# Local attention of a two-layer block: masks added in the pass that takes the maxima, key rotation sum on GpSimd, output product one unit later

## The reference

```python
h = shift_token(x)                       # half of the features from the token before
q, k, v = split(h @ wqkv)                # 8 heads of 64
q = l2norm(q) * qs;  k = l2norm(k) * ksc
q, k = rotary_xpos(q, k)                 # q * cos * scale + rotate_half(q) * sin * scale
# blocks of 128 queries look at 256 keys: their own block and the one before
sim = einsum('bhwid,bhwjd->bhwij', q * 8, k)
mask = (i < j) | (i > j + 128) | (j == -1)
attn = softmax(where(mask, -max, sim))
x = x + (attn @ v) @ wo
```

## Time and profile before

| | |
|---|---|
| median of 3 runs | 3439.26 us |
| the profiled execution's own time | 3436.8 us |
| its span | 3435.1 us |
| PE busy | 3159.2 us, 92% |
| DVE busy | 1936.2 us, 56% |
| ACT busy | 1575.8 us, 46% |
| POOL busy | 724.3 us, 21% |
| mean granted TensorE clock | 0.958 |

### The profile page before, as it was taken

The page is one execution under the profiler, slowest core; times in us unless marked ns, Lnnn a source line. Parts: engine busy times, 40 slices in busy tenths (PEclk is TensorE's granted clock), DMA queues, the critical chain, the costliest instruction groups (busy, mean ns, idle before and its releaser), DMA issues. The chain is left out here.

```text
span 3435.1 us, 46202 instructions
## 1 busy us (share of the span) xinstructions
PE 3159.2 (92%) x15128; PEld 1817.9 (53%) x15129; DVE 1936.2 (56%) x4725; ACT 1575.8 (46%) x3537; POOL 724.3 (21%) x861
## 2 busy tenths in 40 slices
PE   8899998977999969999987999997998999997998
PEld 4455555544666623333324666664555666665555
DVE  6999994541111126666645878773223777775322
ACT  5666652211222226666654666662222656564221
POOL 0000003560000045555532322220001111110111
PEclk9999998998999969999998999998999999998999
DMA  4000004012111111111002000000001000000000
GB/s 145 1 1 1 1 0 167 28 58 92 45 45 44 43 41 28 28 32 30 22 15 65 10 9 10 10 5 27 0 0 34 9 10 8 10 6 4 13 13 25
DMA packets 81274, 97.37 MB, mean 28 GB/s; under 512 B 14611, under 2 KB 68263, under 8 KB 80811
## 3 DMA queue, kind: packets, MB, share of 16 engines
q1 hardware_dynamic: 74106, 76.65, 6.9%
q0 software_dynamic: 6960, 18.10, 1.7%
HBM read 60.35 MB, written 24.13 MB: 25 GB/s over the span
## 5 line engine op out<-in xcount | busy, mean ns | idle before, releaser
L2302 PE MATMUL ps_loc_psa<-sb_stk_w,sb_loc_hT 128*128 128x512 f32 x768 | 350.1, 606 | 5.3 <-DMA sb_stk_wo<-in_loc_wo 3.6
L1706 DVE CUSTOM_DVE_ANT_0 sb_win_masked<-ps_win_pss,sb_win_around 128x384 f32<-128x384 f32 (+1 forms) x512 | 256.3, 538 | 175.0 <-PE ps_win_pss L1801 174.8
L2589 PE MATMUL ps_mlp_ps<-sb_mlp_hT,sb_stk_w 128*128 128x512 f32 (+1 forms) x768 | 322.5, 613 | 22.2 <-DVE sb_mlp_hid L2542 22.2
L2099 ACT ACTIVATE sb_loc_pr<-ps_loc_psw,sb_loc_nb,sb_loc_sc 128x256 f32<-128x256 f32 x512 | 281.0, 569 | 114.4 <-DVE sb_loc_nb L2227 114.4
L1801 PE MATMUL ps_win_pss<-sb_win_kT,sb_win_q 32*128 32x384 f32 (+1 forms) x1024 | 235.2, 531 | 38.1 <-DVE sb_win_qtok L1706 35.7
L1612 ACT ACTIVATE sb_win_pT<-ps_win_pst 128x512 f32<-128x512 f32 x368 | 199.8, 595 | 124.4 <-PE ps_win_pst L1812 122.3
L2542 DVE SCALAR_TENSOR_TENSOR sb_mlp_hid<-ps_mlp_ps,sb_stk_col,sb_mlp_gl 128x512 f32<-128x512 f32 x96 | 71.7, 749 | 303.3 <-ACT sb_mlp_gl L2511 303.3
L2511 ACT ACTIVATE sb_mlp_gl<-ps_mlp_ps,sb_stk_col 128x512 f32<-128x512 f32 x96 | 65.9, 687 | 381.7 <-PE ps_mlp_ps L2589 381.5
L2302 PEld LDWEIGHTS ps_loc_psa<-sb_stk_w,sb_loc_hT 128*128 128x128 f32 x768 | 142.1, 192 | 181.6 <-issue 177.7
L2589 PEld LDWEIGHTS ps_mlp_ps<-sb_mlp_hT,sb_stk_w 128*128 128x128 f32 (+1 forms) x768 | 130.3, 184 | 201.4 <-issue 201.4
L709 PE MATMUL ps_rec_psp<-sb_rec_hT,sb_rec_w 128*128 128x512 f32 x512 | 235.4, 604 | 0.8 <-DVE sb_keep_modf L466 0.8
(11 more groups left out here) (313 smaller groups left out, 6468.1 us busy)
## 6 DMA issues: line engine op xcount, KB each, us to landing
sb_exp_rows<-sorted_tokens SPq DMA_DIRECT2D x72, 128.0 KB, 2.0
expert_results<-sb_exp_res SPq DMA_DIRECT2D x72, 128.0 KB, 1.7
sb_moe_w_in<-in_L_ffn_w_in_eDF SPq DMA_DIRECT2D x8, 512.0 KB, 11.3
sb_moe_w_sw<-in_L_ffn_w_swiglu_eDF SPq DMA_DIRECT2D x8, 512.0 KB, 11.4
sb_exp_w_out<-in_L_ffn_w_out_eFD SPq DMA_DIRECT2D x8, 512.0 KB, 7.1
sb_win_sums<-sb_win_raw SPq DMA_DIRECT2D x128, 32.0 KB, 2.0
sb_stk_angles<-in_angles SPq DMA_DIRECT2D x32, 128.0 KB, 3.8
out_y<-sb_stk_y SPq DMA_DIRECT2D x8, 512.0 KB, 2.9
```

Source lines behind the costliest of these rows:

```text
L1706: nc.vector.tensor_tensor_reduce(masked[:, pair % 2, j, 0:keys], pss[:, (n + j) % PLAIN, 0:keys], around[:, first:first + keys], 1.0, -3e3 ...
L2099: e = nc.scalar.activation(pr[:, hf, h], psw[:, hf, h // 2, h % 2 * 256:h % 2 * 256 + 256], ACT.Exp, scale=sc8[:, b, hh:hh + 1], bias=nb[: ...
L2302: t = nc.tensor.matmul(psa[:, c], hT[:, b, k, 1 - k:P + 1 - k], w[:, k, c * 512:(c + 1) * 512], start=(k == 0), stop=(k == KD - 1))
L2589: i = nc.tensor.matmul(ps[at:at + M, q % 2, i2], w1[:, k, i2 * HID + f * P:i2 * HID + f * P + M], hT[:, b, k], start=(k == 0), stop=(k == ...
```

## The change

Four things are edited, all within `local_attention` and its tiles.

1. `masks` is removed from TensorE, and with it the bf16 identity. The mask is an f32 tile now. `maxima` is one `tensor_tensor_reduce` for each of the four heads of a half: it adds the mask to the scores in PSUM, writes the sum into `pr` in SBUF, and takes the maximum. The exponentials read `pr` and write it in place.
2. The sum of the keys' two rotated parts goes from VectorE (end of `rotate_keys`) to GpSimd (`add_keys`, behind `add_queries`). `rotate_keys(i)` waits for the sum of the tile before.
3. TensorE's `output(i)` moves from behind `turn_keys(i + 1)` to the next tile, between `project(i + 2)` and `turn(i + 1)`.
4. VectorE's `add_output(i)` moves behind `rotate_keys(i + 2)` of the next tile.

```diff
@@ gpsimd
+                def add_keys(i):
+                    j, b, _ = at(i)
+                    pool.wait_ge(s_krot, F + i + 1)
+                    kr = t1[:, b, INNER:]
+                    nc.gpsimd.tensor_tensor(kr, kr, t2[:, INNER:], ALU.add).then_inc(s_krope, 1)
...
                 for i in range(TILES):
                     if i + 1 < TILES:
                         add_queries(i + 1)
+                        add_keys(i + 1)
                     spread_sums(i)
@@ scalar, exps
-                        e = nc.scalar.activation(pr[:, hf, h], psw[:, hf, h // 2, h % 2 * 256:h % 2 * 256 + 256], ACT.Exp,
+                        e = nc.scalar.activation(pr[:, hf, h], pr[:, hf, h], ACT.Exp,
@@ vector, rotate_keys
                     dve.wait_ge(s_k, F + i + 1)
+                    if F + i:
+                        dve.wait_ge(s_krope, F + i)
...
                     i2.then_inc(s_krot, 1)
-                    dve.wait_ge(s_krot, F + i + 1)
-                    kr = t1[:, b, INNER:]
-                    nc.vector.tensor_tensor(kr, kr, t2[:, INNER:], ALU.add).then_inc(s_krope, 1)
@@ vector, maxima
+                    form = 0 if j == 0 else 2 - (j + 1) % 2
                     dve.wait_ge(s_s, n + 1)
-                    nc.vector.tensor_reduce(top[:, hf], psw[:, hf].rearrange("p a (h n) -> p (a h) n", h=2), AX_X,
-                                            ALU.max).then_inc(s_top, 1)
+                    if F + i:
+                        dve.wait_ge(s_tp, n - 1)
+                    else:
+                        dve.wait_ge(s_masks, 16)
+                    for h in range(4):
+                        t = nc.vector.tensor_tensor_reduce(pr[:, hf, h], psw[:, hf, h // 2, h % 2 * 256:h % 2 * 256 + 256],
+                                                           mask[:, form], 1.0, -3e38, ALU.add, ALU.max, top[:, hf, h:h + 1])
+                    t.then_inc(s_top, 1)
@@ vector, loop
                         rotate_keys(i + 1)
+                    if i:
+                        add_output(i - 1)
                     invert_sums(i)
...
                         copy_keys(i + 1)
-                    add_output(i)
...
+                add_output(TILES - 1)
@@ tensor, scores (masks is gone)
                     pe.wait_ge(s_kT, F + i + 1)
+                    if i:
+                        pe.wait_ge(s_riT, F + i)
...
-                                                     kT[r:r + LHD, b, hh // 2].rearrange("p s n -> p (s n)"), start=False,
+                                                     kT[r:r + LHD, b, hh // 2].rearrange("p s n -> p (s n)"), start=(h == 0),
@@ tensor, loop
                         project(i + 1, 2, s_v)
+                    if i:
+                        output(i - 1)
                     turn(i, 0)
...
                         turn_queries(i + 1)
-                        masks(i + 1)
                         turn_keys(i + 1)
-                    output(i)
                     if i + 2 < TILES:
                         turn_input(i + 2)
+                output(TILES - 1)
```

More of the change, by code:

```diff
@@ L1896, in local_attention @@
     ident, x, y, xs_b = keep["ident"], keep["x"], S["y"], S["xs_b"]
-    w, wo, scl, angles, mask, identb = (S[n] for n in ("w", "wo", "scl", "angles", "mask", "identb"))
+    w, wo, scl, angles, mask = (S[n] for n in ("w", "wo", "scl", "angles", "mask"))
     L, sem = layer, S["loc"]
@@ L2017, in _ @@
                 if L == 0:
-                    for dst, name in ((mask, "loc_mask"), (identb, "ident")):
-                        pool.dma_start(dst[:], a[name]).then_inc(s_masks, 16)
+                    pool.dma_start(mask[:], a["loc_mask"]).then_inc(s_masks, 16)
                 nc.gpsimd.memset(v[:, :, 1], 0.0).then_inc(s_pad, 1)
@@ L2030, in _ @@
                 add_queries(0)
+                add_keys(0)
                 tables(1)
@@ L2320, in turn_keys @@
                     t.then_inc(s_kTp, 1)
[L2322 to L2331, removed]
                 def scores(i):
@@ L2394, in _ @@
                 turn_keys(0)
-                if L == 0:
-                    pe.wait_ge(s_masks, 32)
-                masks(0)
                 for i in range(TILES):
@@ L2623, in local_stack @@
             "angles": m.sb("angles", [P, RING, 2, 2, LHD]),
-            "mask": m.sb("mask", [P, 3, 2 * P], BF16),
-            "identb": m.sb("identb", [P, P], BF16),
+            "mask": m.sb("mask", [P, 3, 2 * P]),
             "w": m.sb("w", [P, KD, 3 * INNER]),
```

## The result

The changed kernel takes 3490.72 us (median of 4 runs, 3488.43 to 3496.14), against 3439.57 us for the kernel before on the same chip (4 runs, 3437.61 to 3440.13). The ratio is 1.0152, 95% interval 1.0134 to 1.0170: slower by 51 us, 10 us more than was forecast, and within the range. The profiled execution took 3496.1 us, its span 3494.4 us.

The account below looks back on a forecast made before the run. TensorE's stream was taken as the bound before, the values-to-keys chain after. Thirty steps of +0.78 us (23.4), less 2.2 at the ends, gave 21.2 a layer, 42.4 for two: 3481 us, range 3462 to 3506.

Parts of the forecast that it names:

- The chain from the values' end to usable keys: Behind the values, scaling output and keys, turning and copying keys take 2.97 us; no next scores can start sooner.
- The two idle times: TensorE waits per tile: about 1.0 us ahead of the keys' turn, 0.6 to 0.7 ahead of the scores.
- The step, 16.25, and 16.39 with the additions: Scores to scores in a local-attention tile: 16.25 us against 15.61, 0.64 longer, or 0.78 longer with small terms.
- spreading: GpSimd's spreading of the sums, late behind the output's addition and reciprocal on VectorE, adds 0.06 us a step.
- restart: Scores that start after a wait run slightly longer: 0.08 us a step, bound 0 to 0.2.
- Maxima, exponentials, keys' sum: hidden: First part of a tile: four reductions, exponentials from SBUF and the keys' sum on GpSimd add 0 to the step.
- The ends of a layer, -2.2: Per layer: first scores earlier (-0.86), first step (-0.6), last step's difference (+0.3), last tile (-1); together -2.2 us.
- the first step, -0.6: The first step of a layer has no output in it: 15.0 us for 15.61, so -0.6.
- The last tile, -1: Output falls into TensorE's wait for the last tile's exponentials, and the clock may hold: -1 us, between 0 and -2.5.
- The clock falls at each tile: Rival: two close waits with only turns between cost the full clock, 1.5 us or more a step, 3575; chance 0.08.
- Rival 1, TensorE stays the bound: The saving of 1.04 us a step is kept, step 14.57, total 3372, if the chain is below 2.33; chance 0.08.
- What bounds the kernel now: Local attentions: TensorE, busy for all but 0.4 of 400 us, sets the 15.61 us step; better overlap wins nothing there.

Follow-up runs that it names:

- `masks_only`: Kernel before with only the masks moved to VectorE (in the maxima, no mask products, exponentials from SBUF); ratio 1.0015.
- `out_moved_only`: Kernel before with only the output product and its addition moved to the next tile, masks still on TensorE; ratio 1.0106.
- `out_back`: Changed kernel with the output product and its addition back in their old places; ratio 1.0085.
- `after_again`: Changed kernel, unedited, run once more on another chip; ratio 1.0159 to the kernel before.
- `filler`: Changed kernel with two unused f32 products, about 0.86 us, on TensorE in the wait ahead of the keys' turn; ratio 1.0119 to the kernel before.
- `after_keys_first`: Changed kernel with VectorE scaling the keys ahead of the output; ratio 1.0079 to the kernel before.
- `before_chain_short`: Kernel before, masks still on TensorE, with keys scaled ahead of the output, input turned ahead of the keys, layer 0's normalising late; ratio 0.9960.
- `keys_back`: Changed kernel with only the keys' sum back on VectorE; ratio 1.0146 to the kernel before.
- `after_keys_first_modulate_late`: Changed kernel with keys scaled ahead of the output and, in layer 0, ScalarE's normalising at the end of the tile; ratio 1.0028 to the kernel before.

## Why the prediction was right, point by point

- *The chain from the values' end to usable keys, 2.97 us, becomes the bound.* Right. It is 3.01. `masks_only` and `out_moved_only` show that its two parts are two waits. The keys' turn comes 1.53 us behind the values' end with or without masks, so their removal gains nothing. The scores come at 3.0 to 3.1 once the output no longer stands between, and its move costs the step. The two idle times were forecast as about 1.0 and 0.6 to 0.7 us; they are 0.88 and 0.61.
- *The step, 16.25, and 16.39 with the additions.* It is 16.31. The additions *spreading*, 0.06, and *restart*, 0.08, do not show: the sums' turns follow those of the exponentials after 1.91 as before, and the scores last 1.93. In their place the scores start 0.10 behind the copy, not 0.05. So +0.70 a step, not +0.78.
- *Maxima, exponentials, keys' sum: hidden.* Right for the change: pitch of the reductions 0.35, the exponentials end 1.26 us early. *Keys' sum* is hidden only since the output is ahead of the turns; in `out_back` it costs 0.36.
- *The ends of a layer, -2.2.* Mis-sized. The first scores do come earlier, by 0.77 (0.83 us behind the start of the keys' copy, it was 1.60). But *the first step, -0.6*, is +1.84 in layer 1 and +1.42 in layer 0: its scores run at 1.2 GHz, which costs 1.70 by the rows. The earlier trace rows had been read as scores that could simply start earlier; that the masks ran at the slow clock ahead of them was not seen. That the missing output itself saves what was said is shown by `out_moved_only`, where the masks stand ahead of the scores and the first step is 14.7, 1.66 us under its other steps. *The last tile, -1*: -0.90 in layer 1 from the last scores to the MLP's first transposes, 0.0 in layer 0, where the last scores ran at the slow clock (3.61 for 1.93).
- *The clock falls at each tile* was a rival that excluded the forecast. In truth it is a term of the sum: it falls in 4 steps of 31 a layer in the profiled execution, 6.6 us, and in one and two in `after_again`. This term was left out, because the case was treated as all or nothing. The prediction named a clock below 1.00 in the stretch as a sign of being wrong, and it is 0.99: for this part it was. Whether transposes alone would let the clock fall, as the rival has it, no run separates: `filler` put products where TensorE had been idle.
- *The sum.* Profiled: from the first scores to the last +29.3 and +29.7 us, with the ends +28.5 and +28.0 a layer, 56.5 together; 2.8 of the 59.3 us by which the profiled executions differ lie outside. Forecast 42.4. The difference of 14.1 is clock tiles (+13.2), first steps (+4.5 for the two), smaller steps (-4.8), and ends for the rest. The medians differ by only 51.2; fewer tiles at the slow clock would explain that, as in `after_again`, but the other executions have no trace. That the total is within the range although the clock was left out is in part luck: the range was made of other terms, and the small terms that do not show took back 4.8 us.
- *Rival 1, TensorE stays the bound.* It asked for a chain below 2.33 us. Nothing speaks against the condition: with 2.43, in `after_keys_first`, the step is 15.74, still above 15.61.
- *What bounds the kernel now: nothing can be won by better overlap.* This reading of TensorE's busy time was wrong by 0.23 us a step, as `before_chain_short` shows.

In parts: the masks alone give 1.0015, with the keys' sum on GpSimd 1.0085, with the output's move 1.0152. The output's move alone gives 1.0106.

## What to carry to other kernels

Work that stands between a result and its next use is cover for the chain on the other engines; before removing or moving it, measure the chain from where it starts to where it is awaited, and shorten that chain first. An engine that is busy for 99.9% may still be waiting, for the end of a group in the records can hide a short wait (0.18 us here): look whether another engine's end lies just ahead of a group's start. Short waits that leave the clock alone in most tiles can still cost it in some: count it as a term, not as all or nothing. At the head of a layer whatever stood first behind the wait, the masks or the scores, paid for the slow clock.

## What the runs showed of the hardware

- Two waits of 0.88 and 0.61 us in 16.3, with transposes between, came with a clock of 1.2 GHz in 3, 8 and 10 of 62 steps, by 1.65 us each (`after_again`, the changed kernel, `keys_back`). With the first one filled (`filler`, `out_moved_only`), shortened to 0.29 (`after_keys_first_modulate_late`), or alone (`masks_only`), it never fell between the first step and the last scores, in one profiled execution of each.
- A 128x16 operation of VectorE took 0.73 us beside a GpSimd operation, 0.17 without. In layer 0 of the kernel before it takes 0.70 in 29 of 32 tiles, and no step is longer for it.
- Exponentials with accumulation that read SBUF follow each other after 0.584 us (changed kernel), from PSUM after 0.541 (kernel before).
